# Reordering the first stage and the weight preparation of a four-layer graph network kernel

## The chip, the cores and the metric

The kernel runs on one core of a Trainium2 chip. The metric is the time of one execution in microseconds (us) of device time; lower is better. The engines are named as the profile does: PE (TensorE, matmuls), PEld (its weight loads), DVE (VectorE), ACT (ScalarE), POOL (GpSimd) and SP (SyncE), which issues all transfers.

## The reference

Node features x are 2708 x 512, the adjacency adj is 2708 x 2708, all float32. Four layers follow each other, each with a layer norm and a relu ahead of it and a residual behind it:

```
h = relu(layernorm(x));  x = x + relu(D^-1/2 (adj + I) D^-1/2 @ h @ W0)      # layer 0, D from row sums of adj
h = relu(layernorm(x));  x = x + (D'^-1/2 adj D'^-1/2 @ h) @ W1.T + b1       # layer 1
h = relu(layernorm(x));  x = x + relu(D^-1/2 (adj + I) D^-1/2 @ h @ W2)      # layer 2
h = relu(layernorm(x));  x = x + sigmoid(gate_a * (attn @ (h @ W_sa)) + gate_b * (adj @ (h @ W_gcnb) + b))  # layer 3
```

## The kernel before, in words

**Numbers.** Products are made of float16 halves: a matrix is scaled by a power of two and split into a high half (ACT) and a low half (DVE), and three matmuls (high x high, high x low, low x high) stand for one.

**Tiles and chunks.** The 2708 nodes are 22 tiles of 128 rows (the last has 20). One pass over the adjacency is six chunks of output columns, five of 512 (four tiles) and one of 148 (tiles 20 and 21). Chunk g is aggregated in 22 steps ("agg", g, j), j the tile of source nodes. A step is four groups of three matmuls into four PSUM banks. Chunks 0 to 5 are layer 0. When a chunk is done it is evacuated from PSUM as two halves ("evacuate"), multiplied by the layer's weight ("project"), and its tiles are finished ("post", "moments", "norms", "normed", "hi", "lo").

**One list orders everything.** The function `schedule()` writes one list of stages. Each engine walks through the list and executes its share of every stage, strictly in this order; semaphores make it wait. So what an engine waits for also holds up all that is behind it in its own queue. SP's queue holds every transfer. `plan(u, stage)` puts a stage directly before step u of the step list `SEQ`; `AT[key]` is the position of a step.

**The head.** Layer 0 cannot start before row sums of adj are known. The head is a loop over i = 0 to 25 (line 356). Turn i handles row tile i: "degree" sums a row tile of adj (even tiles on DVE, odd ones on ACT), after which the load of row tile i + 3 is issued ("load_adj", 1354 KB, three buffers, and "load_x"); "moments" takes the statistics of x. Two tiles at a time go through "spread" and "norms"; "h" makes the two halves of h(0,i-3). The step list of the turn (`HEAD[i]`) holds steps of the chunks 0 and 1, also called columns 0 and 1. Column 0 has the step (0,i-4) in turn i. Column 1 begins in turn 9.

**Scales.** Column 0 is scaled by the maximum over rows 0 to 3, column 1 by that over rows 4 to 7, all later chunks by that over all rows. "range" takes the maximum on DVE, which is broadcast over the partitions by a small matmul (line 831) for the first two, by an all-reduce of POOL for the third. "scale" makes the power of two. A column is not split before its scale.

**Splits.** Before each step, `ahead(u)` appends the splits for the steps up to u + 4 and the fetches for the steps up to u + 9. Halves lie in 5 buffers, raw tiles in 5 (8 from chunk 2 on), so split u + 4 waits for step u - 1 and a fetch waits for the split that used its buffer. Where a tile lies on the diagonal of its chunk in layer 0, POOL first adds the identity (line 1550). A split is ACT line 1392 and DVE line 1097.

**Weights.** `weights(u, n)` plans five stages of weight n: the fetch of 1 MB at u, the maximum at u + 3 (DVE line 1154, then an all-reduce on POOL, line 1534), high half at u + 6 and low half at u + 7 for n = 0 and 2 (two later for n = 1, 3 and 4; ACT line 1457, DVE line 1164), and for n >= 3 a store. A stage ("weights", n) planned at a step begins at the step after it. Projection of layer 0 waits for the low half of weight 0. In chunk 5, at step 10, four "restore" transfers of 512 KB bring back halves of h for layer 1; they are in SP's queue between the fetches of (5,18) and (5,19).

Of the kernel before, what the change touches and what calls it, by code (L numbers as in the profile page):

```python
# [17 lines left out]
NT = 22  # L18
# [13 lines left out]
SIX = 4  # L32
START1 = 9
# [4 lines left out]
LA = 4  # L38


HEAD, _next = [[] for _ in range(NT + SIX)], 0
for _i in range(SIX, NT + SIX):
    while _i >= START1 and len(HEAD[_i]) < 2 and _next < _i - SIX:
        HEAD[_i].append(("agg", 1, _next))
        _next += 1
    HEAD[_i].append(("agg", 0, _i - SIX))
# [3 lines left out]
AT = {key: u for u, key in enumerate(SEQ)}  # L50
# [95 lines left out]
class Schedule:  # L146
# [5 lines left out]
    def put(self, kind, *of):  # L152
        self.count[kind] = self.count.get(kind, 0) + 1
        self.no[(kind,) + of] = self.count[kind]
        self.order.append((kind,) + of)
# [5 lines left out]
def schedule():  # L161
    s = Schedule()
    put = s.put
# [5 lines left out]
    def plan(u, *stage):  # L169
        plans.setdefault(u, []).append(stage)  # L170
# [4 lines left out]
    def ahead(u):  # L175
        nonlocal fetched, split, scored, masked
        while scored < len(scores) and AT[scores[scored]] <= u + 6 and scored < masked + 2:
            if not have(("row_out", scores[scored][1])):
                break
            put("score", *scores[scored][1:])  # L180
            scored += 1
        while masked < scored and AT[scores[masked]] <= u + 5 and masked < s.count.get("split_e", 0) + 3:
            if not have(("fetch",) + scores[masked]):
                break
            put("mask", *scores[masked][1:])
            masked += 1
        while split < len(splits) and AT[splits[split]] <= u + LA:
            g, j = splits[split][1:]
            if not have(("fetch", "agg", g, j)) or g < 2 and not have(("scale", g)) or g >= GE and not have(("mask", g, j)):
                break  # L190
            if j < NT - 1 and not have(*freed(user_before("sp", g, j))):
                break
            put("split_e" if g >= GE else "split", g, j)
            split += 1
        while fetched < len(SEQ) and fetched <= u + 9:
            g, j = SEQ[fetched][1:]
            if resident(g, j):
                fetched += 1
                continue
            if j < NT - 1:  # L200
                if not have(*freed(user_before("pair" if GP <= g < GE else "raw", g, j))):
                    break
            elif GP <= g < GE:
                if not have(("agg", g - 2, j)):
                    break
            elif g >= 2 and not have(("mask", g - 2, j) if g >= GE + 2 else ("split", g - 14 if g >= GE else g - 2, j)):
                break
            put("fetch", "agg", g, j)
            fetched += 1

    def fetch_to(n):
        nonlocal fetched
        while fetched < n:
            put("fetch", *SEQ[fetched])
            fetched += 1

    def weights(u, n):
        late = 4 if n in (1, 3, 4) else 2
        for d, kind in ((0, "w_fetch"), (3, "w_max"), (4 + late, "w_hi"), (5 + late, "w_lo"), (11 + late, "w_keep")):
            if kind != "w_keep" or n >= 3:  # L220
                plan(u + d, kind, n)

    def pair(u, l, J):
        nonlocal quiet
        plan(max(later(u, 2.6), u + 1), "norms", l, 2 * J, 2)
        u = max(later(u, 5.2), u + 2, quiet)
        steps = [(0, "normed", l, 2 * J), (0.6, "normed", l, 2 * J + 1), (1.4, "hi", l, J), (2.7, "lo", l, J)]
        if J < 8:
            steps.append((7.9, "image", l, J))
        if l == 1:  # L230
            steps += [(4, "xbias", 2 * J), (4, "xbias", 2 * J + 1)]
        for us, *stage in steps:
            plan(later(u, us), *stage)
        quiet = later(u, 2.7)
        if J == 7:
            for slot in range(4):
                plan(max(later(u, 9.2), AT["agg", 6 * l - 1, 17]), "restore", l, slot, 1)
# [12 lines left out]
    def run(kind, *a):  # L250
        if kind == "norms":
            l, t0, nt = a
            put("norms", *a)
            for t in range(t0, t0 + nt):
                s.no["norms", l, t] = s.count["norms"]
        else:
            put(kind, *a)

    def project(u, g, now):
        p = CHUNKS[g][0]  # L260
        put("project", g, now)
        if p == 4:
            finals(u + 1, g)
            return
        posts(u + 1, p, tiles(g))
        if p == 3:
            plan(later(u + 1, 10.4), "gates", g)
            plan(later(u + 1, 13), "gated", g)

    def step(u):  # L270
        for stage in plans.pop(u, ()):
            if stage[0] == "weights":
                weights(u + 1, *stage[1:])
            elif stage[0] == "pair":
                put("spread", stage[1], 2 * stage[2], 2)
                pair(u, *stage[1:])
            else:
                run(*stage)
        ahead(u)
        put(*SEQ[u])  # L280
        g, j = SEQ[u][1:]
        if g % 6 == 0 and g and j == 3:
            project(u, g - 1, g)
        if j < NT - 1:
            return
        if g >= GE:
            put("row_sum", g)
            put("finish", g)
        else:
            put("evacuate", g)  # L290
        if g % 6:
            project(u, g - 1, g)
# [17 lines left out]
        put("load_adj", t)  # L310
        put("load_x", t)
    put("setup2")
    weights(AT["agg", 1, 9], 0)
    plan(u0 + 1, "constants")
    plan(AT["agg", 2, 3], "gate_w")
    plan(AT["agg", 2, 6], "weights", 4)
    for n in range(8):
        plan(AT["agg", 2, 14] + n, "v_dot", n // 4, n % 4)
    plan(AT["agg", 3, 4], "v_keep")
    plan(AT["agg", 3, 7], "weights", 3)  # L320
    plan(AT["agg", 4, 7], "weights", 1)
    plan(AT["agg", 4, 19], "factors", 1)
    plan(AT["agg", 6, 7], "weights", 2)
    plan(AT["agg", 6, 17], "factors", 2)
    plan(AT["agg", 6, 18], "factors", 3)
# [16 lines left out]
    for t in range(NT):  # L342
        u = AT["agg", 19, 0] + 3 * t
# [12 lines left out]
    for i in range(NT + SIX):  # L356
        if i <= 3:
            fetch_to((0, 3, 5, 5)[i])
        if i in range(2, NT + 1, 2):
            put("spread", 0, i - 2, 2)  # L360
            for n, (t0, nt) in enumerate(((0, 4), (4, 4), (0, NT))):
                if i == t0 + nt:
                    put("range", n, t0, nt)
                    put("scale", n)
        if i == SIX:
            for u in range(-LA, 0):
                ahead(u)
        if 3 <= i < NT + 3:
            put("h", 0, i - 3)
        for key in HEAD[i]:  # L370
            step(AT[key])
        if i in range(2, NT + 1, 2):
            run("norms", 0, i - 2, 2)
        if i < NT:
            put("degree", i)
            if i + 3 < NT:
                put("load_adj", i + 3)
                put("load_x", i + 3)
            put("moments", 0, i)
        if i == NT + 2:  # L380
            put("degrees")
# [31 lines left out]
def gnn_kernel(nc, x, adj, adjT, w0, w1t, b1, w2, wsa, asa, wg, bg, wab1, wab2, bab, out):  # L413
    with ExitStack() as ctx:
# [6 lines left out]
        def hbm(name, shape, dt=F16):  # L421
            return nc.dram_tensor(name, shape, dt).ap()

        s = schedule()
        xs = sb("xs", [P, NT, D])
        HB = sb("HB", [P, 4, 10, 2, 256], F16)
# [1179 lines left out]
```

## Time and profile before

| what | value |
|---|---|
| median of 3 runs | 1857.56 us (1856.84 to 1861.01) |
| profiled execution, its own time | 1859.72 us |
| its span, first to last instruction | 1857.9 us |
| mean granted TensorE clock | 0.991 of full speed |
| PE busy | 1789.2 us |
| DVE, ACT, POOL busy | 911.4, 693.5, 268.6 us |
| head, to the first projection | 157.16 us |

Times in the trace are counted from the span's start. A row of the timeline has the start, the duration, engine and line, the operation with output and input, and in brackets the idle time of the engine before it and what ended it.

### The profile page before, as it was taken

Reading aid. Unit: us, or ns where it says so; the run is one execution under the profiler, and the core shown is the slowest. Engines: PE = TensorE matmul, PEld = TensorE weight load, DVE = VectorE, ACT = ScalarE, POOL = GpSimd, SP = SyncE. Lnnn points to the kernel's source line nnn. Section 1 sums busy time; section 2 is a strip of 40 time slices with the busy share of each in tenths; the row PEclk is TensorE's granted clock in tenths of the full one; section 3 lists DMA queues with packets and bytes.
Section 4 is the critical chain, followed back from the end, with each engine's and each line's share of the span. In section 5 each row is a group of like instructions: output and inputs, shape, how many; then the busy total and the mean of one; then the engine's idle time right before and its main releaser. Section 6 shows DMA issues by size and latency. Waiting matters only on the chain.

```text
span 1857.9 us, 23941 instructions
## 1 busy us (share of the span) xinstructions
PE 1789.2 (96%) x9324; PEld 857.0 (46%) x9324; DVE 911.4 (49%) x1857; ACT 693.5 (37%) x1174; POOL 268.6 (14%) x222
## 2 busy tenths in 40 slices
PE   3989999999999998999999999999999998999998
PEld 1434444454444445444444464444444644444445
DVE  5775755476344443500221132624610567778866
ACT  5664434354332432300121122201100466667656
POOL 0000111021000000000000000301200254455441
PEclk9999999999999999999999999999999999999999
DMA  9974643358655754542323345333332433343323
GB/s 394 361 263 123 181 133 118 101 184 301 209 164 169 231 164 108 164 129 76 110 85 93 99 137 181 102 96 109 100 97 53 131 109 87 108 127 106 114 75 101
DMA packets 158850, 268.98 MB, mean 145 GB/s; under 512 B 34184, under 2 KB 55976, under 8 KB 155516
## 3 DMA queue, kind: packets, MB, share of 16 engines
q1 hardware_dynamic: 158736, 267.45, 46.2%
q8 instruction: 73, 1.20, 0.3%
q14 instruction: 41, 0.34, 0.1%
HBM read 208.79 MB, written 58.59 MB: 144 GB/s over the span
## 4 chain that ended last, share of the span: by engine, by line
PE 86%; DVE 5%; DMA 4%; ACT 3%; issue 2%; SPq 0%; POOL 0%; DVEq 0%; ACTq 0%; POOLq 0%
PE ps L865 23%; PE ps L867 23%; PE ps L866 23%; PE ps L817 16%; PE ps L859 1%; DMA RG<-in_adjT 1%; DMA Ad<-RG 1%; DMA T<-in_adj 1%; DVE T L1111 1%; DVE RG L1097 1%; DMA T<-in_w 1%; ACT T L1406 0%; DVE stage L1311 0%; DMA RG<-Ad 0%; ACT RG L1392 0%
## 5 line engine op out<-in xcount | busy, mean ns | idle before, releaser
L865 PE MATMUL ps<-RG,HB 128*128 128x512 f16 (+1 forms) x2368 | 829.1, 356 | 32.3 <-DVE RG L1097 17.6
L866 PE MATMUL ps<-RG,HB 128*128 128x512 f16 (+1 forms) x2368 | 828.8, 355 | 0.0
L867 PE MATMUL ps<-RG,HB 128*128 128x512 f16 (+1 forms) x2368 | 828.5, 355 | 0.0
L865 PEld LDWEIGHTS ps<-RG,HB 128*128 128x128 f16 x2368 | 233.0, 98 | 272.2 <-DVE RG L1097 20.9
L867 PEld LDWEIGHTS ps<-RG,HB 128*128 128x128 f16 x2368 | 233.0, 98 | 234.6 <-issue 4.2
L866 PEld LDWEIGHTS ps<-RG,HB 128*128 128x128 f16 x2368 | 233.0, 98 | 231.1 <-issue 4.0
L817 PE MATMUL ps<-W,OT 128*128 128x512 f16 (+1 forms) x1320 | 294.0, 382 | 2.3 <-DVE OT L1127 2.3
L1127 DVE SCALAR_TENSOR_TENSOR OT<-ps,OT 128x512 f16<-128x512 f32 (+1 forms) x96 | 53.5, 619 | 385.4 <-ACT OT L1440 385.4
L1097 DVE SCALAR_TENSOR_TENSOR RG<-RG,cS 128x512 f16<-128x512 f32 (+1 forms) x174 | 121.8, 713 | 172.7 <-ACT RG L1392 172.4
L817 PEld LDWEIGHTS ps<-W,OT 128*128 128x128 f16 (+1 forms) x1320 | 129.1, 98 | 162.8 <-issue 9.5
L1580 POOL TENSOR_TENSOR T<-T 128x512 f32<-128x512 f32 (+2 forms) x126 | 169.1, 1342 | 191.5 <-DVE T L1111 190.9
L1440 ACT ACTIVATE OT<-ps 128x512 f16<-128x512 f32 (+1 forms) x96 | 44.7, 551 | 407.4 <-PE ps L859 407.4
L1392 ACT ACTIVATE RG<-RG,cS 128x512 f16<-128x512 f32 (+1 forms) x174 | 114.0, 671 | 178.1 <-PE ps L867 93.1
L1568 POOL TENSOR_SCALAR xs<-xs 128x512 f32<-128x512 f32 (+1 forms) x22 | 39.0, 1778 | 825.0 <-ACT stage L1475 825.0
L1121 DVE TENSOR_TENSOR RG<-T,RG 128x512 f16<-128x512 f32 (+1 forms) x126 | 109.8, 874 | 28.7 <-ACT RG L1430 28.0
L1111 DVE SCALAR_TENSOR_TENSOR T<-RG,T 128x512 f32<-128x512 f32 (+1 forms) x126 | 84.3, 672 | 45.8 <-ACT T L1413 38.8
L1406 ACT ACTIVATE T<-asab,SR 128x512 f32<-128x512 f32 (+2 forms) x132 | 87.6, 667 | 23.7 <-DVE T L1111 23.6
L1097 DVE SCALAR_TENSOR_TENSOR RG<-T,cS,RG 128x512 f16<-128x512 f32 (+1 forms) x78 | 52.7, 685 | 87.0 <-ACT RG L1392 86.8
L1430 ACT CAST RG<-T 128x512 f16<-128x512 f32 (+1 forms) x126 | 70.3, 558 | 48.4 <-PE ps L867 36.2
L1413 ACT ACTIVATE T<-T,DS 128x512 f32<-128x512 f32 (+2 forms) x132 | 86.2, 656 | 0.0
L1392 ACT ACTIVATE RG<-T,cS 128x512 f16<-128x512 f32 (+1 forms) x78 | 50.3, 655 | 88.1 <-PE ps L867 60.0
L1238 DVE CUSTOM_DVE_ANT_0 colb<-stage,Q 128x512 bf16<-128x512 f32 (+1 forms) x88 | 66.1, 751 | 4.1 <-DVE DS L1244 0.4
(189 smaller groups left out, 1123.9 us busy)
## 6 DMA issues: line engine op xcount, KB each, us to landing
RG<-in_adjT SPq DMA_DIRECT2D x253, 256.0 KB, 3.0
RG<-Ad SPq DMA_DIRECT2D x190, 256.0 KB, 2.7
Ad<-RG SPq DMA_DIRECT2D x105, 256.0 KB, 3.3
T<-in_adj SPq DMA_DIRECT2D x14, 1354.0 KB, 8.4
T<-in_adjT SPq DMA_DIRECT2D x62, 256.0 KB, 3.7
HBd<-stage SPq DMA_DIRECT2D x24, 512.0 KB, 3.8
HB<-HBd SPq DMA_DIRECT2D x24, 512.0 KB, 6.5
OT<-in_adj SPq DMA_DIRECT2D x7, 1354.0 KB, 9.2
```

Of the source, the lines that this page charges most:

```text
L817: last = eng.matmul(o, src(i, c), weight(k, c), start=n == 0 and c == 0, stop=n == 2 and c == 3)
L865: eng.matmul(o, h[0], hi, start=j == 0, stop=False)
L866: eng.matmul(o, h[0], lo, start=False, stop=False)
L867: last = eng.matmul(o, h[1], hi, start=False, stop=False)
L1097: eng.scalar_tensor_tensor(lo, raw(g, j), cS[:, n:n + 1], hi, ALU.mult, ALU.subtract).then_inc(s_slo, 1)
L1111: eng.scalar_tensor_tensor(em[0:r, (e - 1) % 3, 0:w], raw(g, j), 0.0, sc_a[0:r, (e - 1) % 2, 0:w], ALU.not_equal, ALU.mult).then_inc(s_mas ...
L1121: eng.tensor_tensor(lo, em[:, (e - 1) % 3, 0:w], hi, ALU.subtract).then_inc(s_elo, 1)
L1392: eng.mul(split_of(g, j)[0], raw(g, j), cS[0:r, n:n + 1]).then_inc(s_shi, 1)
L1406: eng.activation(sc_a[0:r, (e - 1) % 2, 0:w], slrow[0:r, g % 2, 0:w], ACT.Relu, bias=SR[0:r, j:j + 1]).then_inc(s_score, 1)
L1413: eng.activation(o, o, ACT.Exp, bias=bE[0:r, j:j + 1], scale=-0.99).then_inc(s_exp, 1)
L1430: eng.copy(split_of(g, j)[0], em[0:r, (e - 1) % 3, 0:w]).then_inc(s_ehi, 1)
L1580: eng.tensor_tensor(acc[0:r, g % 2, 0:w], acc[0:r, g % 2, 0:w], em[0:r, (e - 1) % 3, 0:w], ALU.add).then_inc(s_acc, 1)
```

## The change

The change reorders stages; the work itself is the same.

- In turns 4 and 5 of the head, the row sum (with the loads that follow it) moves forward: in turn 4 between "range" and "scale" of column 0, ahead of all splits and of h; in turn 5 to the start of the turn, ahead of h.
- In turn 4 only the splits for steps 0 and 1 stand ahead of h(0,1); those for 2, 3 and 4 follow it.
- In turn 8, "range" and "scale" of column 1 move from ahead of h and step (0,4) to behind that step. The splits of column 1 are appended by the first `ahead` that finds the scale, now that of turn 9.
- From turn 22 on, column 1 gets one step in turns 22 and 24 and none in 23 and 25, so that the last steps are (0,19), (1,18), (0,20), (0,21), (1,19), (1,20), (1,21).
- Weight 0 is fetched at step (0,17), in turn 21, instead of (1,9), in turn 13; its maximum is at (0,19), its high half at (0,21), its low half at (1,19).
- Weight 3 begins at (3,14) instead of (3,8): maximum at (3,17) instead of (3,11), halves at (4,0) and (4,1).
- Weight 1 begins at (4,18) instead of (4,8): maximum at (4,21) instead of (4,11), halves at (5,4) and (5,5) instead of (4,16) and (4,17). "factors" 1 follow at (5,18).

```diff
-    while _i >= START1 and len(HEAD[_i]) < 2 and _next < _i - SIX:
+    while _i >= START1 and len(HEAD[_i]) < (2 if _i < NT else 1 - _i % 2) and _next < _i - SIX:
...
-    weights(AT["agg", 1, 9], 0)
+    weights(AT["agg", 0, 17], 0)
...
-    plan(AT["agg", 3, 7], "weights", 3)
-    plan(AT["agg", 4, 7], "weights", 1)
-    plan(AT["agg", 4, 19], "factors", 1)
+    plan(AT["agg", 3, 13], "weights", 3)
+    plan(AT["agg", 4, 17], "weights", 1)
+    plan(AT["agg", 5, 18], "factors", 1)
...
+        def degree():
+            if i < NT:
+                put("degree", i)
+                if i + 3 < NT:
+                    put("load_adj", i + 3)
+                    put("load_x", i + 3)
+
+        ranges = [(n, t0, nt) for n, (t0, nt) in enumerate(((0, 4), (4, 4), (0, NT))) if i == t0 + nt]
+        if i == 5:
+            degree()
         if i in range(2, NT + 1, 2):
             put("spread", 0, i - 2, 2)
-            for n, (t0, nt) in enumerate(((0, 4), (4, 4), (0, NT))):
-                if i == t0 + nt:
-                    put("range", n, t0, nt)
-                    put("scale", n)
+        if i != 8:
+            for n, t0, nt in ranges:
+                put("range", n, t0, nt)
+                if i == 4:
+                    degree()
+                put("scale", n)
         if i == SIX:
-            for u in range(-LA, 0):
+            for u in range(-LA, 2 - LA):
                 ahead(u)
...
         for key in HEAD[i]:
             step(AT[key])
+        if i == 8:
+            for n, t0, nt in ranges:
+                put("range", n, t0, nt)
+                put("scale", n)
         if i in range(2, NT + 1, 2):
             run("norms", 0, i - 2, 2)
+        if i not in (4, 5):
+            degree()
         if i < NT:
-            put("degree", i)
-            if i + 3 < NT:
-                put("load_adj", i + 3)
-                put("load_x", i + 3)
             put("moments", 0, i)
```

## Rows read from the trace of the kernel before

**Rows 1.** The page: busy time and share of the span of each engine.

```profile
PE 1789.2 (96%) x9324; PEld 857.0 (46%) x9324; DVE 911.4 (49%) x1857; ACT 693.5 (37%) x1174; POOL 268.6 (14%) x222
```

**Rows 2.** TensorE's longest later wait: us in total, times, longest us.

```profile
PE ps L865 <- DVE RG L1097: 17.6, 8, 7.7
```

**Rows 3.** Timeline, the scale of column 0 and the first step.

```profile
22.56 0.29 DVE L995 TENSOR_REDUCE cm<-ps 128x1 f32<-128x128 f32 x1 [0.89 <-PE ps L831]
...
25.16 0.61 PE L865 MATMUL ps<-RG,HB 128*128 128x512 f16 x1 [2.63 <-DVE RG L1097]
```

**Rows 4.** Issue of row tile 4, its time to landing, and its sum.

```profile
13.06 0.33 SPq L685 DMA_DIRECT2D T<-in_adj  x1
...
T<-in_adj SPq DMA_DIRECT2D x1, 1354.0 KB, 11.3
...
31.50 1.56 DVE L977 CUSTOM_DVE_ANT_0 T<-T 128x1354 f32<-128x1354 f32 x1
```

**Rows 5.** Timeline, 39 to 50: one h, column 1's broadcast, step 5.

```profile
39.51 0.81 ACT L1340 ACTIVATE Q<-xs,NB,SC 128x512 f32<-128x512 f32 x1 [2.03 <-DVE NB L1046]
40.35 0.62 ACT L1345 CAST HB<-Q 128x512 f16<-128x512 f32 x1
...
41.70 0.66 DVE L1066 TENSOR_TENSOR HB<-Q,HB 128x512 f16<-128x512 f32 x1
...
44.91 0.49 PE L831 MATMUL ps<-identf,colb 128*128 128x128 f32 x2 [3.26 <-DVE colb L988]
...
49.51 0.38 PE L865 MATMUL ps<-RG,HB 128*128 128x512 f16 x1
```

**Rows 6.** Stretches: busy us (instructions) of PE, PEld, DVE, ACT, POOL; clock; DMA.

```profile
45.40:104.00 58.60, 58.60 (x264) 26.07 (x262) 41.51 (x97) 37.05 (x52) 3.75 (x5) 0.97 0.97 369
104.00:121.00 17.00, 11.76 (x53) 4.89 (x53) 12.35 (x29) 10.69 (x14) 0.00 (x0) 1.00 0.81 290
```

**Rows 7.** Timeline, weight 0 on VectorE and ScalarE.

```profile
98.02 2.29 DVE L1154 TENSOR_REDUCE wm<-T 128x1 f32<-128x2048 f32 x1 [2.59 <-DMA T<-in_w]
...
110.35 2.00 ACT L1457 ACTIVATE W<-T,wS 128x2048 f16<-128x2048 f32 x1 [1.92 <-DVE wR L942]
...
113.67 2.34 DVE L1164 SCALAR_TENSOR_TENSOR W<-T,wS,W 128x2048 f16<-128x2048 f32 x1
```

**Rows 8.** Last steps, evacuation 0, first projection; the first row is the chain's.

```profile
153.08 0.88 PE ps L859 x4
...
154.62 2.48 DVE L1127 SCALAR_TENSOR_TENSOR OT<-ps,OT 128x512 f16<-128x512 f32 x4 [0.49 <-ACT OT L1440]
...
157.16 3.17 PE L817 MATMUL ps<-W,OT 128*128 128x512 f16 x10 [2.34 <-DVE OT L1127]
```

**Rows 9.** Timeline, POOL's all-reduce of weight 3 and what follows it.

```profile
265.74 0.38 POOL L1534 PARTITION_ALL_REDUCE wm<-wm  x1 [6.07 <-issue]
273.98 0.44 POOL L1550 TENSOR_TENSOR RG<-RG,identf 128x128 f32<-128x128 f32 x1 [7.86 <-issue]
...
276.07 0.39 PE L865 MATMUL ps<-RG,HB 128*128 128x512 f16 x1 [2.23 <-DVE RG L1097]
```

**Rows 10.** Chunk 5: one stretch, then the timeline of SP and TensorE.

```profile
368.50:388.90 20.40, 17.68 (x258) 17.09 (x257) 12.05 (x38) 12.03 (x28) 0.70 (x2) 0.96 0.73 229
...
374.50 0.33 SPq L712 DMA_DIRECT2D RG<-in_adjT  x1
374.94 2.10 SPq L742 DMA_DIRECT2D HB<-HBd  x4
...
385.94 0.24 PE L865 MATMUL ps<-RG,HB 128*128 128x148 f16 x1 [2.69 <-DVE RG L1097]
```

**Rows 11.** The chain: a later projection; two stretches, clock third from the end.

```profile
224.63 10.36 PE ps L817 x48
...
158.70:162.20 3.50, 3.50 (x10) 1.27 (x9) 2.51 (x5) 0.98 (x2) 0.00 (x0) 0.54 0.77 236
276.00:279.00 3.00, 2.93 (x14) 1.39 (x15) 2.93 (x8) 1.68 (x3) 0.00 (x0) 1.00 0.69 195
```

## The prediction

> **What bounds the kernel now.** The shares come first: TensorE is busy for 96% of the span, VectorE for 49%, ScalarE for 37% [rows 1]. A change that only moves work of the others can win or lose no more than TensorE's pauses and its stretches of low clock. The list of TensorE's waits then says for what: behind the start the low halves of splits (line 1097) lead, 17.6 us in 8 waits [rows 2]. The timeline gives the places: 2.63 us before the first aggregation [rows 3], 3.26 at 44.9, for the broadcast of a maximum [rows 5], 2.34 before the first projection [rows 8], 2.23 at 276 [rows 9], 2.69 at 385.9 [rows 10]. The stretch from 104 to 121 holds 5.24 us of idle TensorE (17.00 less 11.76), and 45.4 to 104 none [rows 6]. A pause can cost twice: after the one at 157 the granted clock is 0.54 for 3.5 us, the lower of its two levels (1.2 GHz), after the one at 276 it stays 1.00 [rows 11]. A matmul of 512 columns takes 0.216 us (10.36 over 48, [rows 11]) and twice that at the low level, so such a stretch loses 1.7 us.
>
> An aggregation step is 12 matmuls, 2.59 us, or 5.2 at the low clock; that of tile 21 is 0.88 [rows 8]. I number the steps of the two first columns from 0: step 5 is (1,0), step 36 is (0,18). Of the changed order I replay the queues with the durations of the rows.
>
> **Part 1: row sum 4 between range 0 and scale 0.** Row 4 is loaded at 13.06 and lands 11.3 us later, at 24.4 [rows 4]. VectorE is ready for scale 0 at 22.56 [rows 3]; now it first waits for the row and sums it (1.5 us to its next instruction, [rows 4]): scale 0 begins at 25.9. From there to the first step it is 2.60 us [rows 3]: that starts at 28.5 instead of 25.16, 3.3 us late. Bounds: if row 4 came with the x tile before it, nothing would be lost; at most 3.4. I take the landing measured.
>
> The steps behind it find their h in time or nearly: h(0,1), which moves ahead of two splits, is ready at 30.3; h(0,2) at 36.1, h(0,3) at 39.5, h(0,4) at 43.7 (each is 0.80 + 0.62 on ScalarE and 0.66 on VectorE [rows 5], behind norms, seven small instructions of 0.2, row sums of 1.5 on VectorE and 2.5 on ScalarE, and moments of 0.8). Row 5's sum, ahead of h(0,2), costs nothing: h(0,2) waits for the norms anyway. Row 7 is fetched 7 us sooner, but its sum stands behind the second half of h(0,4) on ScalarE and ends at 44.9, not 44.1. So step 4 runs from 43.7 to 46.3. Before it ended at 49.51, because the broadcast for column 1 stood before it [rows 5] and the clock was low behind that pause.
>
> **Part 2: range 1 behind step 4.** It hides that broadcast, but the first four splits of column 1, which followed scale 1 at once, now stand in the next turn of the loop. After h(0,5), range and broadcast, scale 1 is there at 49.3; then VectorE has norms 6 and 7 (1.3), row sum 8 (1.5), moments 8 (0.8), the low half of h(0,6) (0.66) and only then the low half of split (1,0) (0.7). Step 5 starts at 54.25, before at 49.51: **4.7 us late**, after 6 us of pause, so at the low clock for some 2 us: 1.05 more (bounds 0 and 2.75).
>
> **Part 3: weight 0 behind the rows.** Before, VectorE waits 2.59 us for this weight, then spends 2.29 and 2.34 on it, ScalarE 2.00 [rows 7], and TensorE loses the 5.24 us of [rows 6] and 1.7 of clock. With this gone I see nothing that starves steps 5 to 35: from 45.4 to 104 the same pattern ran without a pause. DMA share was 0.97 there [rows 6]; it is the thin place. Step 36 started at 137.5 before (157.16 less 2.34, two times 0.88 and six times 2.59). Now: 54.25 + 1.05 + 31 x 2.59 + 0.3 for small pauses = 135.9, **1.6 us early**.
>
> **Part 4: column 0 ends three steps earlier.** The evacuation of column 0 (3.1 us from ScalarE's first copy to VectorE's last) was followed by 0.88 us of TensorE work, hence the 2.34 [rows 8]. Now two full steps and tile 21 (6.1 us) cover it. But weight 0 has come into the same place. From the start of step 36, with VectorE as far ahead as five buffers let it: maximum at 5.7 to 8.0, h(0,21) at 9.3 (needed at 10.4: no pause), two splits, the degrees (some 2.2 us: nine small instructions, a square root on ScalarE and an all-reduce) until 12.9, the weight's scale 13.5, its high half on ScalarE until 15.5, one split, then evacuation 0 from 16.1 to 19.2, and behind that on VectorE the low half of the weight, until 21.5. TensorE is at the projection at 17.3 and waits 4.2. Before, this stretch took 19.6. So the projection starts at 135.9 + 21.5 = 157.4 instead of 157.16: **the head comes out 0.3 us late**, with the same low clock after it. Bounds: the earliest is 17.3 after step 36 (3.9 us early), the latest has a second low stretch behind step 5 (2 late).
>
> **Part 5: weight 3's maximum behind POOL's identities.** POOL's all-reduce begins at 265.74, 6.07 us after its last addition, and the next addition 7.86 us after it; the split of (3,15) waits for that and TensorE 2.23 [rows 9]. Moved to step (3,17), the all-reduce has no addition behind it until 315. **2.2 us won**, no clock. Its other instructions fall into the projection at 292 to 303. The Trainium skill ("GPSIMD Engine Reference", section 2.1) puts the first call of a freshly loaded GpSimd kernel at about 6 us, unseen in the profile; the idle times of 6.07 and 7.86 agree with it, and by its figure the gain would be the same.
>
> **Part 6: weight 1 moves into the narrow chunk.** Before, it stands in chunk 4, where no pause follows. Now fetch and maximum are at (4,18) and (4,21), harmless, but the high half is at (5,4) and the low half at (5,5). Steps of chunk 5 take 0.77 us (2.59 x 148/512), and the splits are four ahead, 3.1 us of cover. Between split (5,7) and split (5,8) ScalarE now waits some 0.9 for the weight's scale and works 2.00 on the weight; between (5,8) and (5,9) VectorE works 2.34 on it [rows 7]. Together 5.2 against 3.1: TensorE starts to wait, some 1.3 before (5,8) and 1.8 before (5,9), and split (5,10) ends 5.1 later (VectorE had 0.1 idle). On that split hangs SP: the fetch of (5,18) at 374.50 waits for its raw buffer, and the four restores of 512 KB at 374.94 and the fetch of (5,19) stand behind that one. TensorE's 2.69 before 385.94 was the wait for (5,19) [rows 10]. All of it moves by 5.1: **5.1 us lost**, low clock as before. Bounds: 0, if the cover holds; 7, if another low stretch falls into work.
>
> "DMA: Bandwidth & Descriptors" of the Trainium skill (section "Anatomy of one DMA") says that a semaphore wait is served on the issuing engine before dispatch; restores at 374.94, directly after that fetch, fit this. By a rule that let restores pass, the sum would be 5.1 lower.
>
> **Sum:** +0.3 - 2.2 + 5.1 = +3.2 us. The profiled execution took 1859.72 (span 1857.9), so 1862.9; the median of the runs shown is 2.2 lower, so **1860.8**.
>
> **Rivals.** (a) *Free restart, faster.* Step 5 starts when step 4 has ended and the broadcast is through, at about 47. Then the head gains 7.4 + 1.05 and the whole is 5.2 faster: 1852.3. For it: VectorE idles before 44. Against: its queue is strictly ordered. It decides if step 5 starts before 48. (b) *The weight hides in chunk 5*: +0.3 - 2.2, 1855.7. For it: VectorE is busy for 12.05 of 20.40 us there [rows 10]; against: the order is by step, not by free time. (c) *More low clock, or DMA short of rows between 90 and 130*: 3.5 to 4 us more, 1864.5. For it: share 0.97 and each new pause can cost 1.7. (d) *Nothing shows*: the pauses were DMA's, 1857.6.
>
> **How the numbers follow.** About 0.2% (3.7 us) is what can be told from no change. My case has 0.52: its own range is 1858 to 1863.5, so 0.32 within 3.7 us of before and 0.20 beyond. (a) 0.15, faster. (b) 0.13 and (d) 0.02, within. (c) 0.18, slower. Together faster 0.15, same 0.47, slower 0.38. The range is 1855 to 1866; it leaves out (a) and the ends of (c).
>
> **What would show it.** First aggregation at 28.5; a TensorE pause of some 6 us ending near 54; no pause between 60 and 130; the weight's low half as the last thing before the first projection; no POOL wait near 275; the restores of chunk 5 issued some 5 us later against the end of projection 3. I am wrong if step 5 starts near 48, or if split (5,10) isn't behind the weight.

## The result: 0.26% slower, and the profile after

| | before | changed |
|---|---|---|
| median of 11 runs each | 1858.45 us (1856.84 to 1862.0) | 1863.69 us (1861.33 to 1866.91) |
| ratio to before | | 1.0026, 95% interval 1.0016 to 1.0035 |
| profiled execution, its own time | 1859.72 us | 1864.49 us |
| its span | 1857.9 us | 1862.6 us |

The change costs 4.8 us by the ratio (3.0 to 6.5) and 4.7 by the spans. I had forecast 3.2 more than before, inside 0.2%; it came out 0.26% slower. (The forecast as a time, 1860.8, was counted from 1857.56, the median of three runs of the kernel before; that of the eleven is 0.9 higher, so 0.9 of the 2.9 us between 1860.8 and 1863.69 is no fault of the sum.) In the page the busy times are as before [rows 1], so nothing was added to the work:

```profile
PE 1788.5 (96%) x9324; PEld 858.0 (46%) x9324; DVE 912.8 (49%) x1857; ACT 693.5 (37%) x1174; POOL 268.8 (14%) x222
```

TensorE is idle for 74.1 us instead of 68.7 (span less busy time), so the difference lies in its pauses. Its list of waits has, after the same two columns of names, the total in us, the number of waits and the longest:

```profile
PE ps L880 <- DVE RG L1112: 26.3, 8, 7.8
...
PE ps L832 <- DVE W L1179: 5.4, 1, 5.4
```

The waits for low halves have grown from 17.6 to 26.3 us [rows 2], and there is a new one, the first projection waiting for the low half of weight 0. Against these 14.1 us stand 8.6 that went: waits for h fell from 6.2 to 2.0, those for broadcasts from 25.0 to 22.9, and the one for the evacuation, 2.3, is gone. The timeline of TensorE gives the places. These are the pauses of more than 1 us from the first aggregation to 392 us:

```profile
28.42 0.61 PE L880 MATMUL ps<-RG,HB 128*128 128x512 f16 x1 [5.90 <-DVE RG L1112]
...
43.57 0.38 PE L880 MATMUL ps<-RG,HB 128*128 128x512 f16 x1 [1.41 <-DVE HB L1081]
47.53 0.49 PE L846 MATMUL ps<-identf,colb 128*128 128x128 f32 x2 [1.22 <-DVE colb L1003]
53.85 0.61 PE L880 MATMUL ps<-RG,HB 128*128 128x512 f16 x1 [5.83 <-DVE RG L1112]
158.88 1.44 PE L832 MATMUL ps<-W,OT 128*128 128x512 f16 x3 [5.41 <-DVE W L1179]
375.75 0.24 PE L880 MATMUL ps<-RG,HB 128*128 128x148 f16 x1 [1.22 <-DVE RG L1112]
378.29 0.30 PE L880 MATMUL ps<-RG,HB 128*128 128x148 f16 x1 [1.60 <-DVE RG L1112]
391.29 0.24 PE L880 MATMUL ps<-RG,HB 128*128 128x148 f16 x1 [3.43 <-DVE RG L1112]
```

The reader is to see what is absent too: nothing between 54 and 158, where 5.24 us were idle before [rows 6], and nothing near 276 [rows 9]. The stretches, with the columns of [rows 6], show the first of these, and the clock at the two long pauses. A low stretch is one in which the granted clock is about half, the lower of the two levels; the windows are set a little wider, so they show 0.51 or 0.52:

```profile
50.80:57.60 6.80, 3.75 (x10) 1.41 (x11) 5.61 (x10) 3.99 (x7) 0.00 (x0) 0.52 0.91 347
60.00:150.00 90.00, 90.00 (x418) 40.59 (x417) 65.70 (x165) 61.23 (x86) 3.20 (x7) 1.00 0.78 274
156.60:163.40 6.80, 4.52 (x12) 1.69 (x13) 6.76 (x12) 2.41 (x5) 0.00 (x0) 0.51 0.36 102
```

Measured against before at fixed points: the first projection starts 1.72 us later (158.88 against 157.16), the first aggregation behind it 2.1 later (171.35 against 169.21). Chunk 5 starts 0.3 earlier (368.20 against 368.46), so 2.4 have been won in between. The step (5,19) starts 5.35 later (391.29 against 385.94), and the end of the span 4.7 later. Behind (5,19) all kernels of this document have the same schedule, and yet the profiled executions take from 3.7 us less to 1.2 more there than the one of before: their low stretches hold between 8.4 and 16.8 us of TensorE's work, and those with less are the faster ones. So the traces below are compared at fixed points up to (5,19), and not by their spans.

Three more views carry the account by parts. VectorE in turns 8 and 9, between the broadcast and the first split of column 1:

```profile
48.83 0.14 DVE L957 TENSOR_SCALAR cR<-cE 128x1 uint32<-128x1 uint32 x1
...
50.16 1.56 DVE L992 CUSTOM_DVE_ANT_0 OT<-OT 128x1354 f32<-128x1354 f32 x1
...
52.47 0.66 DVE L1081 TENSOR_TENSOR HB<-Q,HB 128x512 f16<-128x512 f32 x1
53.05 3.40 DVE L1112 SCALAR_TENSOR_TENSOR RG<-RG,cS 128x512 f16<-128x512 f32 x5
```

Scale 1 is there at 49.0; the row sum, the moments and the low half of h stand before the low halves of the splits, which begin at 53.05. Second, weight 0 at the end of the head:

```profile
142.60 2.28 DVE L1169 TENSOR_REDUCE wm<-T 128x1 f32<-128x2048 f32 x1
...
150.68 2.00 ACT L1472 ACTIVATE W<-T,wS 128x2048 f16<-128x2048 f32 x1 [2.40 <-DVE wR L957]
153.20 2.03 ACT L1455 ACTIVATE OT<-ps 128x512 f16<-128x512 f32 x4
154.00 2.48 DVE L1142 SCALAR_TENSOR_TENSOR OT<-ps,OT 128x512 f16<-128x512 f32 x4
156.39 2.34 DVE L1179 SCALAR_TENSOR_TENSOR W<-T,wS,W 128x2048 f16<-128x2048 f32 x1
```

The evacuation ends at 156.5 and the weight's low half behind it at 158.7. Third, chunk 5, VectorE, ScalarE and SP:

```profile
372.14 2.00 ACT L1472 ACTIVATE W<-T,wS 128x2048 f16<-128x2048 f32 x1 [0.94 <-DVE wR L957]
...
375.33 0.36 DVE L1112 SCALAR_TENSOR_TENSOR RG<-T,cS,RG 128x148 f16<-128x148 f32 x1
375.61 2.35 DVE L1179 SCALAR_TENSOR_TENSOR W<-T,wS,W 128x2048 f16<-128x2048 f32 x1
377.87 0.37 DVE L1112 SCALAR_TENSOR_TENSOR RG<-RG,cS 128x148 f16<-128x148 f32 x1
...
379.79 2.12 SPq L757 DMA_DIRECT2D HB<-HBd  x4
```

The low half of weight 1 stands between two splits, and the restores are issued at 379.79 instead of 374.94 [rows 10].

### The profile page after: what moved, and what is told of

It is laid out like the page before. It is cut to its first block, busy times and chain, and to the rows that moved or that the text cites. A ratio compares the mean times of both kernels' runs of the same rounds, so it can differ in the third digit from the quotient of the medians.

```text
span 1862.6 us, 23939 instructions
## 1 busy us (share of the span) xinstructions
PE 1788.5 (96%) x9324; PEld 858.0 (46%) x9324; DVE 912.8 (49%) x1857; ACT 693.5 (37%) x1174; POOL 268.8 (14%) x222
## 4 chain that ended last, share of the span: by engine, by line
PE 86%; DVE 5%; ACT 3%; DMA 3%; issue 1%; SPq 0%; DVEq 0%; POOL 0%; ACTq 0%
PE ps L880 23%; PE ps L881 23%; PE ps L882 23%; PE ps L832 16%; PE ps L874 1%; DMA T<-in_adj 1%; DMA Ad<-RG 1%; DVE T L1126 1%; DVE RG L1112 1%; ACT RG L1407 0%; ACT T L1421 0%; DVE stage L1326 0%; DMA RG<-in_adjT 0%; DMA RG<-Ad 0%; ACT T L1428 0%
## 5 line engine op out<-in xcount | busy, mean ns | idle before, releaser
L880 PE MATMUL ps<-RG,HB 128*128 128x512 f16 (+1 forms) x2368 | 830.7, 356 | 36.7 <-DVE RG L1112 26.3
L1445 ACT CAST RG<-T 128x512 f16<-128x512 f32 (+1 forms) x126 | 70.3, 558 | 48.5 <-PE ps L882 36.3
L1407 ACT ACTIVATE RG<-T,cS 128x512 f16<-128x512 f32 (+1 forms) x78 | 50.5, 655 | 97.7 <-PE ps L882 65.7
```

What stands on the lines that cost most here:

```text
L880: eng.matmul(o, h[0], hi, start=j == 0, stop=False)
L1407: eng.mul(split_of(g, j)[0], raw(g, j), cS[0:r, n:n + 1]).then_inc(s_shi, 1)
L1445: eng.copy(split_of(g, j)[0], em[0:r, (e - 1) % 3, 0:w]).then_inc(s_ehi, 1)
```

## The experiments

Every ratio below is against the kernel before, run beside it on the same chip; the kernels fall into three groups on three chips, and the changed kernel itself was measured apart from them. The table lists them in the order of the sections; the last column is the difference in us by the ratio. By their ratios two of these kernels can be told apart only if some 2.5 us lie between them, 3.2 where the intervals are wider (an estimate, from the intervals of the two). Where less lies between, the trace has to decide, and where it can't, the text says so.

| kernel | ratio, 95% interval | median us | us |
|---|---|---|---|
| changed, weight 1 back | 1.0006 (0.9997 to 1.0015) | 1858.87 | +1.1 |
| before, only weight 1 moved | 1.0021 (1.0013 to 1.0030) | 1862.6 | +3.9 |
| before, only weight 3 moved | 0.9983 (0.9974 to 0.9992) | 1856.81 | -3.2 |
| changed, row sums back | 1.0024 (1.0014 to 1.0034) | 1862.43 | +4.5 |
| changed, range 1 back | 0.9992 (0.9983 to 1.0001) | 1857.67 | -1.5 |
| changed, splits behind scale 1 | 1.0013 (1.0004 to 1.0022) | 1860.78 | +2.4 |
| changed, weight 0 back | 1.0028 (1.0016 to 1.0040) | 1863.24 | +5.2 |
| changed, weight 0 two turns sooner | 1.0015 (1.0006 to 1.0024) | 1861.46 | +2.8 |
| changed, order of last steps back | 1.0032 (1.0021 to 1.0043) | 1864.38 | +5.9 |
| combined | 0.9953 (0.9940 to 0.9965) | 1849.58 | -8.7 |
| combined, weight 0 spread | 0.9969 (0.9957 to 0.9981) | 1853.95 | -5.8 |

### Weight 1, alone and taken back

The first kernel is the changed one with weight 1 where it was:

```diff
-    plan(AT["agg", 4, 17], "weights", 1)
-    plan(AT["agg", 5, 18], "factors", 1)
+    plan(AT["agg", 4, 7], "weights", 1)
+    plan(AT["agg", 4, 19], "factors", 1)
```

> The changed kernel with weight 1 back in chunk 4 (begun behind (4,7), factors 1 at (4,19)); all else as changed. My theory: the halves of weight 1 between the narrow steps cost TensorE its pauses at 374 to 378 and hold split (5,10), behind which the four restores and the fetch of (5,19) wait. So the restores come about 5 us earlier, TensorE goes on with (5,19) at some 386 instead of 391.3, and the kernel takes 5.4 us less than the changed one: about 1858.3, like the kernel before. Rival (the restores are late for another cause, such as the state of the queues after the head): the wait before (5,19) still ends near 391 and the time stays at 1863.7.

It takes 1858.87 us against the 1859.02 of before beside it, ratio 1.0006. The two pauses of 1.22 and 1.60 are gone, and the wait for the fetch behind the restores is nearly what it was before [rows 10]:

```profile
386.57 0.31 PE L880 MATMUL ps<-RG,HB 128*128 128x148 f16 x1 [2.78 <-DVE RG L1112]
```

The second is the reverse: the kernel before, with only weight 1 moved (the two lines the other way round).

> The kernel before with weight 1 alone moved, to behind (4,17), factors 1 to (5,18). My theory: the same pauses before (5,8) and (5,9) and a restore 5.3 us later as in the changed kernel, so 5 us more than before: 1863.8. Rival (it costs that only together with the other edits, because VectorE comes late into chunk 5): 1860 or less.

It is 3.9 us slower by its ratio (2.4 to 5.6), with the pauses of the changed kernel, and (5,19) 3.7 later than in [rows 10]. Its chunk 5 had begun 0.7 earlier, so across the chunk it lost 4.4:

```profile
375.28 0.24 PE L865 MATMUL ps<-RG,HB 128*128 128x148 f16 x1 [1.22 <-DVE RG L1097]
377.83 0.24 PE L865 MATMUL ps<-RG,HB 128*128 128x148 f16 x1 [1.60 <-DVE RG L1097]
...
389.66 0.24 PE L865 MATMUL ps<-RG,HB 128*128 128x148 f16 x1 [2.01 <-DVE RG L1097]
```

So the move of weight 1 costs by itself, without any other part. My rival (b), that it hides, falls. Eight of the traces have this move, and their chunk 5 takes 21.8 to 23.1 us from its start to (5,19); the three traces with weight 1 in its old place take 17.5 to 17.6. In all thirteen (5,19) starts 10.2 to 11.7 us after the first restore is issued, wherever that is, which fits the path through SP's queue. No run moved the restores alone.

### Weight 3 alone

The kernel before with one line changed, `plan(AT["agg", 3, 13], "weights", 3)`.

> The kernel before with weight 3 alone moved, to behind (3,13). My theory: POOL's all-reduce comes after the identities of chunk 3, the pause of 2.23 us at 276 goes, nothing else changes: 2.2 us less than before, 1856.3. Rival (the fetch of the tile, not POOL, was late): the pause stays and the time is that of before, 1858.5.

It is 3.2 us faster (1.5 to 4.8), and the pause of [rows 9] is gone. In the trace 2.40 us are won between the first aggregation behind projection 0 and chunk 5, and (5,19) starts 2.56 us before the 385.94 of [rows 10]:

```profile
383.38 0.24 PE L865 MATMUL ps<-RG,HB 128*128 128x148 f16 x1 [2.69 <-DVE RG L1097]
```

The span of this execution is 6.2 us shorter, but the other 3.6 are luck: it is the fastest of its eleven runs, and they arise behind (5,19), 2.1 of them near 1104, where it has no low stretch and the kernel before has one. The size that I gave, 2.2, lies in the interval.

The trace also shows what held POOL before. At 259.9 and at 266.1 its sequencer has a MODIFY_POOL_CONFIG; from the first it is 5.8 us to the all-reduce, from the second 7.9 to the next addition [rows 9]. The prediction lets both idle times agree with one figure; the way back took 2 us more than the way there. In the changed kernel the first stands at 262.9, right behind the last addition, and the all-reduce begins at 282.50, 0.14 us after its maximum is ready (280.08 and 2.28). There POOL has nothing else to do, and the same work delays nobody.

### The row sums back

The changed kernel with every `degree()` at the end of its turn:

```diff
-        if i == 5:
-            degree()
...
-                if i == 4:
-                    degree()
...
-        if i not in (4, 5):
-            degree()
+        degree()
```

> The changed kernel with row sums 4 and 5 back at the end of their turns; range and scale of column 1 stay behind step (0,4). My theory: the first step starts at 25.2 instead of 28.4, but step 5 hangs on row sum 7 on ScalarE (loaded three rows behind) and on VectorE's queue, so it comes out at about 53.5 instead of 53.85, and the kernel takes only 0 to 1 us less: 1863.2. Rival (the late first step is what makes the head late): step 5 starts 3 us earlier, at about 50.8, and the time is 1860.5.

The first step starts at 25.23 as before, yet step 5 starts at 53.78, against 53.85 in the changed kernel:

```profile
25.23 0.61 PE L875 MATMUL ps<-RG,HB 128*128 128x512 f16 x1 [2.63 <-DVE RG L1107]
...
47.15 0.80 PE L841 MATMUL ps<-identf,colb 128*128 128x128 f32 x2 [3.11 <-DVE colb L998]
53.78 0.61 PE L875 MATMUL ps<-RG,HB 128*128 128x512 f16 x1 [5.83 <-DVE RG L1107]
```

The 3.2 us by which part 1 delays the first step are gone again at step 5: TensorE stands still before 47 and again before 54 for other reasons. The ratio, 1.0024 against 1.0026, agrees. The clock doesn't quite: in this trace, behind the pause of 3.11, it is low from 46.3 to 59.9, with 6.9 us of work in it against 3.75 in the changed kernel, and the first aggregation behind the projection comes 1.55 us later. It is the slowest of its nine runs (1866.95, their median 1862.43), so whether the early row sums save clock stays open.

### Range and scale 1 back, and only the splits moved

Two kernels ask what the late step 5 costs. In one, range and scale 1 of the changed kernel return to ahead of h in turn 8:

```diff
-        if i != 8:
+        if True:
...
-        if i == 8:
-            for n, t0, nt in ranges:
-                put("range", n, t0, nt)
-                put("scale", n)
```

> The changed kernel with range and scale of column 1 back ahead of h(0,5) and step (0,4), so that the first splits of column 1 stand in turn 8 again. My theory: step 5 hangs on where these splits stand. TensorE waits some 2 to 3 us for the broadcast at 45, step (0,4) follows, and step 5 starts at 48.5 to 50 instead of 53.85. The head is 4 to 5 us shorter and the whole 1859.2. Rival (step 5 hangs on the late start, whichever way the broadcast stands): step 5 still starts near 53 and the time is 1863.

In the other they stay behind step (0,4), but one line appends the splits of column 1 directly behind the scale:

```diff
             for n, t0, nt in ranges:
                 put("range", n, t0, nt)
                 put("scale", n)
+            ahead(AT["agg", 0, 4])
```

> The changed kernel with one call more: the splits that scale 1 allows are appended directly behind it, in turn 8, ahead of norms 6, row sum 8 and moments 8. Range and scale stay behind step (0,4), rows 4 and 5 stay early. My theory: the lateness of step 5 is the queue of VectorE between scale 1 and the first split; step 5 starts at about 50.5 instead of 53.85, the pause before it is some 2.5 us instead of 5.83, and the time is 3.3 to 5 us less than the changed kernel's, 1859.5. Rival (step 5 waits for row sum 8 or a transfer): it still starts at 53.8, 1863.7.

The first came out at 0.9992, 6.3 us below the changed kernel (1.0026 less 0.9992, times 1858), more than the 4.5 that I expected, though its step 5 starts at 51.02 and not between 48.5 and 50. Its timeline has the old pause for the broadcast, and behind it the splits at once, with the first projection at 154.08 instead of 158.88:

```profile
45.32 0.79 PE L842 MATMUL ps<-identf,colb 128*128 128x128 f32 x2 [3.19 <-DVE colb L999]
...
47.15 2.56 ACT L1403 ACTIVATE RG<-RG,cS 128x512 f16<-128x512 f32 x4 [0.74 <-DVE cR L953]
...
51.02 0.52 PE L876 MATMUL ps<-RG,HB 128*128 128x512 f16 x1
...
154.08 12.00 PE L828 MATMUL ps<-W,OT 128*128 128x512 f16 x48 [5.19 <-DVE W L1175]
```

The second has step 5 at 50.84, where I expected 50.5, 3.0 earlier than in the changed kernel:

```profile
47.75 0.49 PE L847 MATMUL ps<-identf,colb 128*128 128x128 f32 x2 [1.22 <-DVE colb L1004]
50.84 0.61 PE L881 MATMUL ps<-RG,HB 128*128 128x512 f16 x1 [2.60 <-DVE RG L1113]
```

Its first projection starts at 156.52, 2.4 earlier, and 1.0013 is 2.4 us below the changed kernel, just at the edge of what the ratios can tell and less than the 3.3 to 5 that I expected. So the queue between scale 1 and the splits makes the late step 5, as the prediction said. But both kernels bring step 5 forward by about the same (to 51.02 and 50.84), and only the first gains 4.8 at the projection. The rest is the clock. From step 5 to step 36 the first takes 80.4 us, the second 83.1, the changed kernel 82.0, and 31 steps at full speed are 80.3. In the first the low stretch (44.7 to 51.6) holds the broadcast and step 4 and ends as step 5 begins; in the second it (49.9 to 56.7) holds 5.9 us of the steps behind step 5.

### Weight 0 in four places

With weight 0 back at (1,9) in the changed kernel (`weights(AT["agg", 1, 9], 0)`):

> The changed kernel with weight 0 back at (1,9), in turn 13. My theory: the wait of 5.4 us before the first projection (for the low half of weight 0) and one low stretch of clock go, 6 to 7 us; the pauses between 104 and 121 (5.2 us and one low stretch, 7 us) come back. So the time is about the same, 1863.7 to 1865, and TensorE goes from step (1,21) to the projection without a pause. Rival A (DMA made those pauses, not the weight's work): no pauses come back and the time is 1857 to 1858. Rival B (the evacuation makes the wait before the projection): a pause over 2 us stays there and the time is 1867 or more.

The pauses of [rows 6] return, the one before the projection goes, and the ratio is 1.0028. The ratios show no difference between the two places, and the first aggregation behind the projection comes only 0.8 us later:

```profile
119.66 0.39 PE L880 MATMUL ps<-RG,HB 128*128 128x512 f16 x1 [1.10 <-DVE RG L1112]
126.01 0.59 PE L880 MATMUL ps<-RG,HB 128*128 128x512 f16 x1 [3.59 <-DVE HB L1081]
```

Two turns sooner than in the changed kernel (`weights(AT["agg", 0, 15], 0)`), so that its low half is ahead of evacuation 0:

> The changed kernel with weight 0 begun at (0,15) instead of (0,17): still behind all row loads, but with its low half at (0,19), ahead of the degrees and of evacuation 0. My theory: the pause of 5.41 us before the first projection was VectorE's queue of degrees, evacuation and low half; it goes, with some 2 us of low clock: 1857 to 1858, if h(0,21) isn't late in turn (a pause of up to 1 us). Rival (ScalarE and VectorE have no time left in the last turns, wherever the weight stands): pauses of the same sum appear before the steps (0,20) and (0,21) and the time stays at 1863.

Here I was wrong and the rival largely right. Nothing waits before the projection, but 4.9 us of pause stand further ahead, against 5.41:

```profile
140.80 0.38 PE L880 MATMUL ps<-RG,HB 128*128 128x512 f16 x1 [2.02 <-DVE HB L1081]
...
149.03 0.38 PE L880 MATMUL ps<-RG,h 128*128 128x512 f16 x1 [2.89 <-DVE h L1084]
```

The ratio, 1.0015, is 2.0 us below that of the changed kernel, less than the ratios can tell apart. In the trace the first aggregation behind the projection is 0.8 us earlier: the pauses fell by 0.5, and the low stretches of the head hold some 1 us less of work.

The fourth place is in the combined kernel (last heading of this section) with its four stages drawn apart over turns 15 to 21:

```diff
-    weights(AT["agg", 0, 15], 0)
+    for at, kind in ((22, "w_fetch"), (26, "w_max"), (30, "w_hi"), (33, "w_lo")):
+        plan(at, kind, 0)
```

> The combined kernel (before's turns 4, 5 and 8, column 0 ends first, weights 3 and 1 behind (3,13) and (4,13)) with weight 0 laid out over four turns: fetch at step 22, maximum at 26, high half at 30, low half at 33. My theory: each part alone (2.3, 2.0, 2.3 us) is smaller than the lead of four steps, and between them VectorE makes up about 0.75 us a turn, so the pauses of 0.6 and 2.9 us and the low stretch behind them shrink: 2 to 4 us less than the combined kernel, 1846. Rival (VectorE has no time to make up, a weight anywhere in these turns costs the same): 1849.6 or more, with the pauses near 125 to 140.

My theory fell here too: 0.9969 against 0.9953 for the kernel that it was to better. The ratios alone don't tell these two apart (3.0 us, on two chips), but in the traces the first aggregation behind the projection is 3.9 us later. Its pauses are the largest of the four places, 6.2 us in sum, and the low half of the weight comes just behind a row sum on VectorE:

```profile
126.59 0.38 PE L866 MATMUL ps<-RG,HB 128*128 128x512 f16 x1 [1.90 <-DVE HB L1067]
...
128.99 1.56 DVE L978 CUSTOM_DVE_ANT_0 OT<-OT 128x1354 f32<-128x1354 f32 x1
...
131.87 2.35 DVE L1165 SCALAR_TENSOR_TENSOR W<-T,wS,W 128x2048 f16<-128x2048 f32 x1
...
132.10 0.38 PE L866 MATMUL ps<-RG,HB 128*128 128x512 f16 x1 [0.17 <-DVE HB L1067]
...
139.01 0.58 PE L866 MATMUL ps<-RG,HB 128*128 128x512 f16 x1 [4.15 <-DVE HB L1067]
```

So the sums of the pauses are 5.2 us at (1,9) before the change, 5.4 at (0,17), 4.9 at (0,15) in the changed kernel but only 3.5 in the combined one, and 6.2 drawn apart. The weight is 2.28 + 2.34 us of VectorE and 2.00 of ScalarE, 6.6 together; wherever it was put, half of that or more came back as pauses of TensorE. At (0,15) and (0,17) all row tiles have been requested before the weight is fetched, so there its work makes the pauses; at (1,9), where VectorE also waited 2.59 us for the transfer [rows 7], no run parts the two.

### The order of the last steps back

The changed kernel with the old rule, `len(HEAD[_i]) < 2`, so that columns 0 and 1 alternate to the end.

> The changed kernel with the step order of before (the columns alternate to the end). Weight 0 stays late, its low half now ahead of evacuation 0 on VectorE. My theory: the three steps of cover were spent on a queue that the weight had filled; without them evacuation 0 ends some 3.5 us after its first copy and the projection starts 1 to 2 us sooner than in the changed kernel (at about 157.5, pause 3 us): 1862. Rival (the cover is worth the 2.34 us that the evacuation cost before): the projection starts 2 us later, 1866.

Neither of my two numbers: 1864.38, ratio 1.0032. The 1.1 us above the changed kernel are less than the ratios can tell; the trace says 0.6 (159.45 against 158.88), and 0.2 at the first aggregation behind it. Here the weight's low half comes first and the evacuation is last:

```profile
153.32 2.35 DVE L1179 SCALAR_TENSOR_TENSOR W<-T,wS,W 128x2048 f16<-128x2048 f32 x1
...
156.91 2.48 DVE L1142 SCALAR_TENSOR_TENSOR OT<-ps,OT 128x512 f16<-128x512 f32 x4
...
159.45 3.17 PE L832 MATMUL ps<-W,OT 128*128 128x512 f16 x7 [6.18 <-DVE OT L1142]
```

The two pieces, 2.35 and 2.48 on VectorE, swap places, and TensorE waits for both in either order. The earlier end of column 0 is worth nearly nothing while weight 0 stands behind it.

### A combined kernel

The parts that looked good are put together: the kernel before with the new order of the last steps, weight 0 at (0,15), weight 3 moved as in the change, and weight 1 moved only to where its high half falls on (5,0).

```diff
-    while _i >= START1 and len(HEAD[_i]) < 2 and _next < _i - SIX:
+    while _i >= START1 and len(HEAD[_i]) < (2 if _i < NT else 1 - _i % 2) and _next < _i - SIX:
...
-    weights(AT["agg", 1, 9], 0)
+    weights(AT["agg", 0, 15], 0)
...
-    plan(AT["agg", 3, 7], "weights", 3)
-    plan(AT["agg", 4, 7], "weights", 1)
-    plan(AT["agg", 4, 19], "factors", 1)
+    plan(AT["agg", 3, 13], "weights", 3)
+    plan(AT["agg", 4, 13], "weights", 1)
+    plan(AT["agg", 5, 18], "factors", 1)
```

> The kernel before, turns 4, 5 and 8 as they were, with what the earlier runs speak for: column 0 ends three steps ahead, weight 0 begun at (0,15), weight 3 behind (3,13), weight 1 behind (4,13), so that its high half stands at (5,0) under the projection of chunk 3, factors 1 at (5,18). My theory: first projection at some 148 instead of 157.2 (5.24 + 1.7 of pauses and low clock, 2.3 of the handover), 2.2 for weight 3, chunk 5 as before: 11 us less than before, about 1847. Rival (the gains overlap, DMA becomes the bound in turns 13 to 18): 1852 or more, with pauses between 90 and 130.

It takes 1849.58 us, ratio 0.9953 (0.9940 to 0.9965), 8.7 us faster than before, where I expected 11. It beats both kernels. Its first projection starts at 152.50, where I expected 148: I had counted weight 0 as free at (0,15), and 3.5 us of pause and a low stretch stayed. There is no pause before the projection; the longest of the head behind step 5, and the one in chunk 5, are

```profile
141.35 0.58 PE L865 MATMUL ps<-RG,h 128*128 128x512 f16 x1 [2.89 <-DVE h L1069]
...
377.92 0.30 PE L865 MATMUL ps<-RG,HB 128*128 128x148 f16 x1 [3.42 <-DVE RG L1097]
```

Here the handover pays, since nothing but the evacuation stands in it: neither the 2.34 of [rows 8] nor the 5.4 of the changed kernel is left. In the trace the first aggregation behind the projection is 6.35 us earlier than before, 2.4 are won up to chunk 5 by weight 3, and chunk 5 takes 0.7 longer, so that nothing speaks for the move of weight 1.

## Why the prediction was right in its steps and short in its sum

**Parts 1 and 2, held.** First step at 28.42 (predicted 28.5), step 4 at 43.57 (43.7), step 5 at 53.85 (54.25) after 5.83 us of pause (6). The row sums back show the first delay absorbed; range 1 back and the splits behind scale 1 show that the second one counts and that the queue between scale and splits makes it. The clock behind it cost more than the 1.05 I put: from step 5 to step 36 it is 1.7 us more than 31 full steps. Rival (a), the free restart, is refuted: it asked for a step 5 before 48, and the earliest with part 2 in it, with the splits right behind the scale, came at 50.84.

**Part 3, held, its number by luck.** There is no pause from 60 to 150, and step 36 starts where I said, at 135.9:

```profile
135.88 0.38 PE L880 MATMUL ps<-RG,HB 128*128 128x512 f16 x1
```

That it fits to the tenth is luck: step 5 came 0.4 early, the clock took 0.7 more than its term, and the 0.3 for small pauses was not needed. With the weight taken back the pauses return.

**Part 4, the step that was mis-sized.** The mechanism is as predicted: VectorE's queue has the weight's low half behind evacuation 0, and it is the last thing before the projection. I put its end at 21.5 us after step 36, and it came 22.9 after; the pause was 5.41 instead of 4.2. Most of the delay is already in the high half on ScalarE, which ended 16.8 after step 36 instead of 15.5. And I had "the same low clock after it": the low stretch is 6.8 us long (156.6 to 163.4) against 3.5 before [rows 11]. Of it, 2.3 us fell into the pause and 4.5 into work, 1 more than before, which costs 0.4 to 0.5. Head in sum: +2.1 at the first aggregation behind the projection, where I had +0.3. Of the 1.8 missing, about 1.5 are between step 36 and the projection, and the rest is clock behind it. The upper bound that I kept for part 4 (2 us late) holds the projection, 1.7 late, but by another way than the one I gave for it.

**Part 5, held.** The pause of 2.23 is gone; 2.4 us were won from the first aggregation to chunk 5 (predicted 2.2), and alone it gives 3.2 (1.5 to 4.8).

**Part 6, held.** Pauses of 1.22 and 1.60 (1.3 and 1.8), restores 4.85 later (5.1), (5,19) 5.35 later. Alone the move costs 3.9 by time (2.4 to 5.6) and 4.4 across chunk 5 in its trace; over the eight traces that have it the chunk takes 4.3 to 5.6 more than the 17.5 of before, and 5.1 lies among them. The kernel before has one low stretch in chunk 5, 387.4 to 390.9. The changed kernel has two: 378.5 to 381.9, right behind the new pauses, and 392.1 to 395.6. The first of these,

```profile
378.50:382.00 3.50, 3.50 (x33) 3.50 (x32) 2.85 (x10) 1.69 (x6) 0.00 (x0) 0.55 0.50 122
```

holds 3.5 us of busy TensorE at the lower level, 1.2 GHz. "Low clock as before" was therefore wrong, but it mattered little: the work of that stretch stands ahead of the wait for (5,19), which SP's queue sets. Four traces have the same two pauses and no low stretch behind them, and there too the chunk takes 4.3 to 5.1 more.

**The sum.** By the trace: +2.1 in the head, -2.4 up to chunk 5, +5.6 across chunk 5, -0.6 for the rest, 4.7. Predicted were +0.3, -2.2, +5.1. One term, part 4, took the time from within 0.2% to beyond it. The chances didn't allow for it enough: of my own case 0.32 was put within 0.2% and 0.20 beyond, though the forecast lay only 0.5 us inside that line and the head had bounds of 3.9 early and 2 late.

**What stays open.** The runs by time don't quite add up to the trace. The changed kernel less its weight 1 is +1.1 us and weight 3 alone -3.2, which leaves 4.3 for the head, where the trace shows 2.1. The intervals (about 1.7 to either side of each) hold both, so neither is shown. Why weight 0 costs 3.5 us of pauses at (0,15) in the combined kernel and 4.9 in the changed one, I did not find. And what sets whether a pause is followed by a low stretch, and of what length, no run here shows.

## What to carry to other kernels

In a schedule with a fixed order, price a stage that is moved by what stands behind it in each engine's queue, not by the free share of the engine: weight 1 cost 3.9 us between steps of 0.77 us, though VectorE had over 40% free there, because the 0.9 us of waiting for its scale and two pieces of 2.00 and 2.34 us were more than the 3.1 us that the four splits in hand could cover. When a wait is hidden by moving its start, move also all that its end lets go: scale 1 lost its gain because its splits stayed a turn behind; one line made the pause 3.2 us shorter. And where two engines feed a third with little to spare, work that is moved about comes back as pauses: 3.5 to 6.2 us here for 6.6 us of work. The gains here came from places with real cover (the all-reduce in a stretch without additions, the evacuation behind two full steps).

## What the hardware showed that I had not expected

The low clock doesn't come in one size. Behind pauses of 3.26 and 2.34 us the kernel before had stretches of 3.4 to 3.5 us at the lower level. Behind the 5.83 us at step 5 of the changed kernel, and the 5.41 before its projection, they were 6.8 us. Yet with range 1 back, a single pause of 3.19 us before the broadcast was also followed by a long one:

```profile
44.70:51.60 6.90, 6.28 (x16) 2.59 (x17) 5.43 (x20) 4.09 (x7) 0.00 (x0) 0.52 1.01 419
```

With the row sums back, where a pause of 3.11 and one of 5.83 follow each other, it was 13.6 us. And a pause need not be followed by any: eight traces have the same pauses of 1.22 and 1.60 in chunk 5, and the clock fell behind them in four (changed, only weight 1 moved, range 1 back, order of last steps back) and not in the four others. Weight 0 two turns sooner is one of these:

```profile
377.50:381.00 3.50, 3.26 (x44) 2.76 (x45) 2.88 (x8) 1.46 (x5) 0.00 (x0) 1.00 0.46 108
```

So neither the length of the pause nor the order of the work alone decides it. A prediction should keep 0 and the 6.9 us as bounds for a new pause, and one trace of each kernel can't show a difference of 2 us that rests on the clock.
